# Rests of GpSimd in place of landing waits among indirect transfers, and twenty shared-expert units ahead of the expert blocks

## What is computed

```python
x = layernorm(x + retention(x))                 # layer 0: 8 heads, decayed causal
x = layernorm(x + cross_attention(x, ctx))      # 16 heads of 16
x = layernorm(x + moe64(x))                     # 64 experts 256->64->256, top 8, and 2 shared experts 256->512->256
x = layernorm(x + linear_memory_attention(x))   # layer 1
x = layernorm(x + cross_attention(x, ctx))
x = layernorm(x + moe8(x))                      # 8 gated experts 256->512->256, top 2
```

## Time and profile before

| | us |
|---|---|
| median of 3 runs | 2316.37 |
| lowest, highest | 2305.85, 2327.61 |
| the profiled execution, its own time | 2324.08 |
| its span in the trace | 2322.0 |
| PE busy | 1859.6 (80%) |
| DVE busy | 1173.1 (51%) |
| POOL busy | 779.4 (34%) |
| ACT busy | 627.4 (27%) |

### The profile page before, as it was taken

One profiled execution on the slowest core, in us unless ns is written; L12 is line 12 of the kernel. 1 busy time (PEld: TensorE's weight loads), 2 busy tenths in 40 slices (PEclk: granted clock), 3 DMA queues, 4 the chain that ended last, 5 costly groups with the idle time before them and its releaser, 6 DMA issues. The chain is left out here.

```text
span 2322.0 us, 49333 instructions
## 1 busy us (share of the span) xinstructions
PE 1859.6 (80%) x19787; PEld 1461.6 (63%) x19787; DVE 1173.1 (51%) x3042; ACT 627.4 (27%) x957; POOL 779.4 (34%) x899
## 2 busy tenths in 40 slices
PE   4898888897685399967677853898998849999994
PEld 2676666565553177645455642676777649999994
DVE  4465555464332044566544433576756534556654
ACT  0232222131220055533333521333333211111110
POOL 0004434533544400355555226444222220222223
PEclk9998888797687699978798976887788869999997
DMA  9213442542548566776767763222310041233332
GB/s 308 98 43 131 155 143 78 171 140 96 178 154 202 168 196 219 249 231 218 224 219 224 241 211 92 81 65 69 124 38 29 29 162 51 71 98 94 101 94 66
DMA packets 269647, 322.84 MB, mean 139 GB/s; under 512 B 25083, under 2 KB 245487, under 8 KB 268655
## 3 DMA queue, kind: packets, MB, share of 16 engines
q1 hardware_dynamic: 236399, 227.38, 31.1%
q0 software_dynamic: 33024, 92.32, 12.3%
HBM read 157.22 MB, written 162.40 MB: 138 GB/s over the span
## 5 line engine op out<-in xcount | busy, mean ns | idle before, releaser
L1399 POOL DMA_INDIRECT big<-results,slots x256 | 256.7, 1003 | 368.2 <-DMA results<-e_y 149.7
L2024 PE MATMUL wide<-d_xt,d_ws 128*128 128x128 f32 x2272 | 278.9, 276 | 0.6 <-issue 0.6
L2024 PEld LDWEIGHTS wide<-d_xt,d_ws 128*128 128x128 f32 x2272 | 272.6, 193 | 4.5 <-issue 1.0
L578 POOL DMA_INDIRECT lists<-big,slots x160 | 155.2, 970 | 143.8 <-DMA lists<-big,slots 85.0
L832 DVE RECIPROCAL rden<-bank 128x256 f32<-128x256 f32 x64 | 112.3, 1755 | 146.7 <-PE bank L1169 105.2
L640 ACT ACTIVATE pt<-wide 77x2048 f32<-77x2048 f32 x64 | 120.0, 1875 | 239.4 <-PE wide L1157 192.1
L1685 PE MATMUL wide<-e_xt,e_w1s 128*64 128x128 f32 x1280 | 103.2, 312 | 91.3 <-DVE e_w1s L1590 88.1
L1414 DVE SCALAR_TENSOR_TENSOR big<-big,weights 128x256 f32<-128x256 f32 x256 | 106.9, 480 | 125.2 <-DMA big<-results,slots 104.4
L110 PE MATMUL wide<-shared_sx,shared_sw 128*128 128x512 f32 x256 | 136.6, 659 | 23.4 <-DMA shared_sx<-res_t 20.8
L1685 PEld LDWEIGHTS wide<-e_xt,e_w1s 128*64 128x64 f32 x1280 | 81.0, 156 | 107.3 <-DVE e_w1s L1590 96.0
L127 PE MATMUL wide<-shared_sw,shared_sh 128*128 128x256 f32 x512 | 123.0, 384 | 16.0 <-DVE big L1654 16.0
(11 more groups left out here) (275 smaller groups left out, 3690.2 us busy)
## 6 DMA issues: line engine op xcount, KB each, us to landing
lists<-zero SPq DMA_DIRECT2D x20, 2048.0 KB, 14.3
e_x<-lists SPq DMA_DIRECT2D x80, 512.0 KB
results<-e_y SPq DMA_DIRECT2D x80, 512.0 KB
d_x<-lists SPq DMA_DIRECT2D x71, 128.0 KB
results<-d_y SPq DMA_DIRECT2D x71, 128.0 KB
e_w<-in_L_w SPq DMA_DIRECT2D x2, 4096.0 KB, 38.8
x<-in_x SPq DMA_DIRECT2D x8, 512.0 KB, 5.3
shared_sw<-in_x_t SPq DMA_DIRECT2D x32, 128.0 KB, 3.1
```

The costliest lines, as they stand in the source:

```text
L578: pool.indirect_dma_start(out=lists, out_offset=bass.IndirectOffsetOnAxis(ap=slots[:, b, i, k:k + 1], axis=0), in_=z2[i % 3][:, b, :], in_ ...
L1399: pool.indirect_dma_start(out=picked[:, c % NG, b, :], out_offset=None, in_=results[0:-(-PAGES_OF_STEP[s] // 4) * 4 * R0, :], in_offset=ba ...
L2024: ins = mm(out[T % 2][:, a * P:(a + 1) * P], ws[:, T % NW, n, c, a * P:(a + 1) * P], xt[:, T % 2, c], start=c == 0, stop=c == KC - 1)
```

## The change

A helper `Rest` is added. The first call fills a small array with ones; each call then issues one power operation of POOL on 128x4 elements and waits for it. Three places call it in place of a landing wait: the "put" of step 6 (`STEPS - 2`, 6 places), the scatters of the last step (8 places, the first of which had no wait before), and each gather group but the first (63 places). The waits of the readers (DVE's for a gathered group, SP's for all scatters) stay, as does the wait for the add four groups back. `FIRST_UNITS` goes from 12 to 20. The two `load_w2` move from ahead of `load_route(0)` to behind the load of step 2's `shared_sx`, at the first unit of `feed_order` (number 8).

```diff
+class Rest:
+    def __init__(self, nc, ctx, link):
+        self.nc, self.link, self.begun = nc, link, False
+        self.ones = ctx.enter_context(nc.sbuf_tensor("rest_ones", [P, 2, NB], F32))
+
+    def __call__(self, pool):
+        step = Step(pool, self.link)
+        if not self.begun:
+            self.begun = True
+            step(self.nc.gpsimd.memset(self.ones[:], 1.0))
+        step(self.nc.gpsimd.tensor_tensor(self.ones[:, 1], self.ones[:, 0], self.ones[:, 0], ALU.pow))
...
                     for b in range(NB):
-                        if b:
+                        if b and i == STEPS - 2:
+                            shared.rest(pool)
+                        elif b:
...
-FIRST_UNITS = 12
+FIRST_UNITS = 20
...
             if c:
-                pool.wait_ge(got[(c - 1) % NG], 16 * NB * ((c - 1) // NG + 1))
+                shared_sems.rest(pool)
             if c >= NG:
                 pool.wait_ge(summed, c - NG + 1)
...
             load_rows(0)
-            load_w2(0)
-            load_w2(1)
...
                     experts.load_rows(sp, src_t, shared)
                     shared += 1
+                    if n == UNITS:
+                        load_w2(0)
+                        load_w2(1)
...
                 for k in range(K0):
-                    if k % 4 == 0 and b + k:
-                        pool.wait_ge(put, 16 * (b * K0 + k))
+                    if k % 4 == 0:
+                        shared_sems.rest(pool)
...
+        shared.rest = Rest(nc, ctx, shared.pool_step)
```

## The result

The changed kernel takes **2237.12 us** (median; 2316.37 before), a ratio of 0.9651 with an interval of 0.9611 to 0.9692: about 80 us less, against 71 forecast. The ratio leaves out one disturbed run of the changed kernel (2262.71 us), which the median of five runs still holds; the mean of the other four is 2235.8 us. The profiled execution took 2246.83 us with a span of 2244.8, 77.2 less than before.

| stretch, by its two marks | before | after | difference | forecast |
|---|---|---|---|---|
| start to the first scatter of step 6 (code that didn't change) | 683.6 | 693.1 | +9.5 | 0 |
| to the first block on PE | 127.2 | 125.3 | -1.8 | -2 |
| to the first gather | 144.3 | 141.6 | -2.6 | 0 |
| to the sum in block 65 | 324.7 | 283.3 | -41.3 | -45 |
| to layer 1's first memset on POOL | 81.5 | 58.1 | -23.4 | -20 (tail 15, end 5) |

The account below looks back on a forecast made before the run. No engine was full: in the gather stretch POOL's gather loop paced DVE and DVE paced PE, 8.17 us a group. Terms 2 + 45 + 15 + 5 + 4 = 71 us gave 2245 us, 8-in-10 range 2215 to 2296.

Parts of the forecast that it names:

- late bound: Before the first block: the second add to base comes at 780 at the latest, within 765 to 780, 772 taken.
- buy no more than this: Before the first block: rests among the scatters win only 2 us, between 9 won and 8 lost.
- The 5 us taken off for longer landings: Gathers, blocks 24 to 65: deduction for longer landings at a transfer share of 0.86, leaving 45 us won.
- the ordinary row: Gathers: a rest priced at the usual 1.02 us for a power on 128x4, though 1.29 occurred once.
- the rule's reading: Gathers: by the shared SBUF interfaces each rest would cost 0.3 us more, 12 us less won; not used in the sum.
- the floor of the working: Tail, blocks 66 to 79: transfers allow a block no less than 3.3 us; 3.8 was taken, 15 us won.
- from step 1 on, POOL's gathers are off the path: Layer 1: POOL's gathers matter only up to the first norm scale, 4 us won (0 to 8).
- A: Rival: transfer engines become the bound at 260 GB/s, period 7.15 us, 46 won, 2270 us; chance 0.18.
- B: Rival: the landing wait only moves, gather period stays near 8 us, 23 won, 2293 us; chance 0.16.
- C: Rival: unpaced gathers and scatters hold up block loads and stores; at period 9.0, 28 us lost, 2344 us; chance 0.09.
- 1.3 us for a rest: Gathers: a rest puts about 1.3 us between two transfers where the plain gap is 0.30; period 6.65, 6.8 taken.
- D: Rival: too many units ahead, first block 8 us late, 61 won, 2255 us; chance 0.57 together with the forecast.

Follow-up runs that it names:

- scatter_rests: The kernel before with rests among the scatters of steps 6 and 7 alone (14 places); 2136.97 us, ratio 0.9871 to the kernel before.
- units_only: The kernel before with 20 units ahead of the blocks and weight loads behind step 2's inputs, all landing waits kept; 2132.7 us, ratio 0.9858.
- late_waits: The changed kernel with landing waits back for the 18 gather groups behind the first three of layer 1; 2244.22 us, ratio 0.9699 to the kernel before.
- gathers_add_rest: The changed kernel with an add on 128x4 instead of the power as rest among the gathers; 2051.93 us, ratio 0.9490 to the kernel before.
- gathers_bare: The changed kernel with neither rest nor landing wait among the gathers, scatters keeping their rests; 2295.2 us, ratio 0.9906 to the kernel before.

## Why the prediction was right, step by step

**The first block (2 forecast, 1.8 measured).** Right in its mechanism; that the number came so close is in part luck. The last scatter ended 96.7 us after the first began, against the 95.4 of the working. PE's idle time moved ahead of unit 17's outward and is set by the second add, 85.3 us after the first scatter (86.2 before); the forecast wanted 88 and had 96 as its late bound. From the add to the first block it took 40.0 us instead of the 36 of the working: PE began 1.35 us after the add, and its first outward took 3.78 us and the next inward 2.54 where later ones took 1.89 and 1.88 (the granted clock of 779.7 to 818.4 was 0.94). The 3 us sooner and the 4 us longer nearly cancel. That the rests "buy no more than this" was right in kind and too low in size: the scatters' rests alone win 26 us (`scatter_rests`), and behind the 20 units 7. The prediction had applied the rule of the Trainium skill on queues that take turns (DMA: Bandwidth & Descriptors, Queues, rings and completion order) and got the late bound for the add from it; the trace doesn't bear that out here. Counted from the first scatter, the store was issued after 69.2 us instead of 73.3, and the load behind it was issued 12.1 us later instead of 9.5, so what the freed scatters took stayed below what the sooner store gave.

**The gathers (45 forecast, 41.3 measured; 41 alone in another set).** Right in its mechanism, with one term off: the period is 283.33 / 40 = 7.1 us, not 6.8. The 5 us taken off for longer landings were not needed for that reason, since POOL never came to wait for the add four groups back, but they covered most of the longer period. A rest took 1.19 us on average beside the sums and up to 1.88; the other 37 of the same profile took 39.4 / 37 = 1.06. So the ordinary row was too low a price for a power there. The Trainium skill's rule of the SBUF interfaces that GpSimd shares with VectorE (GPSIMD Engine Reference, Specifications) speaks for such a stretch; the runs show the size, about 0.13 us a rest beside the sums, 5 us in all, where the rule's reading had 12. Transfers issued beside DVE rose from 1.015 to 1.058 us each, 7 us more in all; the prediction had named transfers longer than 1.0 us as a sign of being wrong, and this one showed, though small. Transfers ran at 260 GB/s and 0.81, as forecast in kind (274 and 0.86).

**The tail and the end (20 forecast, 23.4 measured).** Right. Up to the end of ACT's last result the tail is 16.1 us shorter (15 forecast), and from there to layer 1 it is 7.2 (5 forecast). The 16.1 is made otherwise than forecast: a block took 3.3 us, the floor of the working, rather than 3.8, which would have won 22, but 11.6 us of PE's waits for staged weights stand in the tail (one of 9.44 at its start), against 7.3 before. `units_only` shows it alone: 56.6 us, where it is 82.3 without this part.

**Layer 1.** The first stretch gave 2.0 of 4 us. Not forecast were the 13.6 us between the first and the sixth norm scale. The granted clock was 0.85 instead of 0.78 in them. Where the kernel before takes 2317 us this stretch sorts by rests or none, and less well by the clock (`late_waits`, above), so the prediction's step "from step 1 on, POOL's gathers are off the path" was probably wrong by 6 or 7 us here and the clock gave what is left; in the first and third set it held. Against it stand 9.5 us lost before the first scatter in unchanged code, where that mark lies anywhere from 676.8 to 693.1 in executions of the second set and these runs. Without these two stretches the others add up to 73.1 us, against 71 forecast; that the whole span came out close owes something to their cancelling.

**The rivals.** *A* (transfers the bound, 7.15 us a group) named the period that was measured, but not its cause: `gathers_add_rest` ran at 285 GB/s with 0.88, so 260 was no ceiling. *B* (the wait only moves) is refuted: a second rest costs 0.9 us a group, which a hidden pause would not. Its counter-argument was misread, though: of the 42 waits up to the gather at 1298.11 only 12 lie between 1.97 and 2.18 us, and 26 are longer, so "most are 2.0 us" doesn't hold. *C* (gathers that nothing holds back stall the others) did not happen, because one short rest is enough; with the rest gone as well it happened nearly as described, though not to a time above that of the kernel before. What the prediction missed in it: the rest has a part in the gain of its own. It counted the rest as a cost only, and the step "1.3 us for a rest" would by its logic have made no rest at all the better kernel by some 40 us (40 x 1.0); it was 58 us the worse. *D* had no 8 us: the first block wasn't late.

## What to carry to other kernels

A wait for landing among indirect transfers that nobody needs for correctness (the readers here have waits of their own) can be replaced by a short operation of the engine that issues them, but not by nothing: measure the bare version, a short and a long pause side by side, since here 0.3 us was better than 1.2 and both better than none. When two parts of a change fill the same gap (here sooner scatters and more units), add up their gains by the gap, not by the parts. Behind large loads on one queue the next issue stands until they are nearly through; put there what is needed last.

## What the runs showed of the hardware that was not expected

- Gathers issued back to back by GpSimd (0.95 us each, 0.30 between) held up the other engines: PE's matmuls came with holes of 0.5 to 1 us, 30.3 us in one stretch against 0.5, and ACT and DVE had waits of up to 15.9 us that ended 1.2 to 2.9 us after GpSimd's last gather of a run (three places in `gathers_bare`). One operation of 0.3 us with its completion after each four removed that: the 40 groups took 257.3 us (`gathers_add_rest`) instead of 324.0 (in different sets).
- The issue behind 8 MB of loads on SP's queue took 24.1 to 24.6 us here and 25.1 before, whichever transfer it was.
- The same kernel took 2316 and 2318 us in two sets and 2161 and 2163 in two others. In the changed kernel's two profiles 129 of some 169 us lie before the first scatter (693.11 and 564.19). From 173 to 693 the granted clock was 0.75 to 0.82 in the one, and from 140 to 564 it was 0.86 to 0.96 in the other. The first and the second set (2163 and 2318) carry the same chip number, the third (2161) another, so the chip number doesn't sort them; what else lowers the clock, no run shows.
